# SyncE gathers seven tiles of each edge stage row by row

## The reference, cut to what matters

```python
k = typed_linear(x, ntype, Wk).reshape(n, H, HS)      # q and v alike
k_j, q_i, v_j = (k[src], q[dst], v[src])
kw = rel_apply(k_j, etype, Watt)                      # per head and relation, 16x16
a = (kw * q_i).sum(-1) * pri[:, etype].T / SQRT_D
amax = jax.ops.segment_max(a, dst, num_segments=n)
ex = jnp.exp(a - amax[dst])
den = jax.ops.segment_sum(ex, dst, num_segments=n)
alpha = ex / (den[dst] + 1e-16)
m = rel_apply(v_j, etype, Wmsg)
agg = jax.ops.segment_sum(alpha[..., None] * m, dst, num_segments=n)
out = jax.nn.silu(typed_linear(agg.reshape(n, HID), ntype, Wa))
```

## Time and profile before

| | |
|---|---|
| median of 3 runs | 2782.73 us (2780.76 to 2786.0) |
| profiled execution | 2787.17 us, span 2785.5 us |
| GpSimd busy | 1945.5 us (70%), 2030 instructions |
| VectorE busy | 2357.5 us (85%), 5622 instructions |
| TensorE busy | 1628.5 us (58%) |
| ScalarE busy | 1296.0 us (47%) |
| first and last gather, layer 0 | 348.57 and 1328.33 us |
| first and last gather, layer 1 | 1600.28 and 2578.16 us |

### The profile page before, as it was taken

How to read it: one execution, slowest core, us unless ns; L and a number is a source line. 1 busy time by engine, 2 the same in 40 slices (tenths; PEclk the granted TensorE clock), 3 DMA queues, 4 the chain that set the end, 5 groups by cost and what they waited for, 6 DMA issues and landing times. The chain is left out here.

```text
span 2785.5 us, 49119 instructions
## 1 busy us (share of the span) xinstructions
PE 1628.5 (58%) x11035; PEld 1427.7 (51%) x11035; DVE 2357.5 (85%) x5622; ACT 1296.0 (47%) x4592; POOL 1945.5 (70%) x2030
## 2 busy tenths in 40 slices
PE   1967645555555555555577645555555555556466
PEld 1855535555555555454455545555554555555344
DVE  7977679888898888888578689888898888988588
ACT  0037614444444444444577724444444444444455
POOL 2636677777777777777377677777777777777276
PEclk6569968777778787877699967787778777777655
DMA  5539876666666666665267776666666666665311
GB/s 135 89 139 355 326 226 191 186 182 185 187 181 186 184 184 185 184 185 166 75 272 276 281 219 184 186 184 185 186 184 186 184 185 184 184 183 161 126 47 37
DMA packets 386053, 512.90 MB, mean 184 GB/s; under 512 B 74933, under 2 KB 297835, under 8 KB 373268
## 3 DMA queue, kind: packets, MB, share of 16 engines
q0 software_dynamic: 101952, 328.62, 38.0%
q1 hardware_dynamic: 274712, 179.39, 21.7%
q10 hardware_dynamic: 9104, 1.86, 0.4%
HBM read 382.63 MB, written 142.96 MB: 189 GB/s over the span
## 5 line engine op out<-in xcount | busy, mean ns | idle before, releaser
L1248 POOL DMA_INDIRECT g_rows<-node_kv,edge_key_sb x1564 | 1481.5, 947 | 483.1 <-issue 442.7
L1426 ACT ACTIVATE acc<-g_ps_sum 128x127 f32 x1564 | 414.8, 265 | 851.3 <-DVE g_gained L1360 720.0
L1430 ACT ACTIVATE acc<-acc,g_gained,g_scale x1564 | 600.0, 384 | 2.1 <-issue 1.2
L1487 PE MATMUL g_ps_q<-g_qw,g_hot_t 128*128 128x128 f32 x3128 | 544.2, 327 | 83.3 <-DMA g_qw<-node_q 48.2
L1476 PE MATMUL g_ps_sum<-g_hot,g_rows 128*128 128x128 f32 x3128 | 565.6, 338 | 1.4 <-ACT acc L1430 1.4
L1487 PEld LDWEIGHTS g_ps_q<-g_qw,g_hot_t 128*128 128x128 f32 x3128 | 496.5, 239 | 96.3 <-DMA g_qw<-node_q 49.4
L1476 PEld LDWEIGHTS g_ps_sum<-g_hot,g_rows 128*128 128x128 f32 x3128 | 535.6, 256 | 2.0 <-ACT acc L1430 1.9
L1282 DVE TENSOR_TENSOR g_rows<-g_rows,g_ps_q 128x512 f32<-128x512 f32 (+1 forms) x446 | 256.9, 618 | 96.2 <-DMA g_rows<-node_kv,edge_key_sb 95.0
L1496 PE MATMUL g_ps_a<-ident,g_score 128*112 128x128 f32 x112 | 51.4, 459 | 418.4 <-DVE g_score L1287 418.4
L1496 PEld LDWEIGHTS g_ps_a<-ident,g_score 128*112 128x112 f32 x112 | 18.8, 168 | 443.6 <-DVE g_score L1287 443.6
L1262 DVE TENSOR_TENSOR g_hot_t<-g_rank_row,g_ps_a 128x1792 f32<-128x1792 bf16 x112 | 224.7, 2006 | 23.8 <-DMA g_rank_row<-edge_rank 23.5
(11 more groups left out here) (249 smaller groups left out, 2872.4 us busy)
## 6 DMA issues: line engine op xcount, KB each, us to landing
g_qw<-node_q SPq DMA_DIRECT2D x1564, 64.0 KB
g_rank_row<-edge_rank SPq DMA_DIRECT2D x110, 448.0 KB
g_rows<-node_kv,edge_key_sb POOLq DMA_INDIRECT x1564, 3.2
node_agg<-n_agg SPq DMA_DIRECT2D x24, 256.0 KB, 2.3
node_rows<-node_x SPq DMA_DIRECT2D x2, 1792.0 KB
node_q<-l_blank_q SPq DMA_DIRECT2D x1, 3200.0 KB
node_q<-n_q_sb,node_slot POOLq DMA_INDIRECT x112
node_kv<-n_kv,node_id POOLq DMA_INDIRECT x112
```

What stands on the lines that cost most here:

```text
L1248: g_.indirect_dma_start(out=rows[b % U][:, g, :], out_offset=None, in_=scratch["kv"][:, :], in_offset=bass.IndirectOffsetOnAxis(ap=tab["ke ...
L1426: a.activation(acc[:, bass.ds(w + 1, P - 1)], ps_sum[q % BANKS][:, n, 1:P], ACT.Copy).then_inc(s["copied"], 1)
L1430: a.activation(at, at, ACT.Identity, scale=scale[b % 2][:, 0, g:g + 1], bias=gained[q % BANKS][:, n:n + 1]).then_inc(s["joined"], 1)
L1487: ins = t.matmul(ps_q[q % BANKS][:, n, :], hot_t[b % 2][:, g, :], qw[b % 2][:, g, :], start=True, stop=True)
```

## The change

In each edge stage seven tiles, the last (tile 13) of batches 6, 14, 22, 30, 38, 46 and 54, are no longer gathered by GpSimd. SyncE fetches their rows one DMA per row, 128 x 7 = 896 DMAs of 1 KB for a layer, with addresses from registers: 40 rows in batch 0, 16 in each batch after it, and 8 in batch 54. The rows go to two tiles of their own (`far0`, `far1`); when a tile is complete, SyncE copies it into its place in `rows` with one more DMA, at the start of the following call of `batch`. VectorE's product of tiles 12 and 13 waits for that copy in those batches.

The keys of the seven tiles and a second copy of the window starts are put in partitions 64 and 32 of `window_starts_sb` in the tables stage, and GpSimd scales them there to offsets in bytes. SyncE's query DMAs now use the byte offsets and a view of `node_q` as bytes.

```diff
@@ tables stage, SyncE @@
-                sp.dma_start(tab["w0"][:, :], scratch["w0"].rearrange("(p w) -> p w", p=1)).then_inc(s["rows_in"], 16)
+                sp.dma_start(tab["w0"][0:1, :], scratch["w0"].rearrange("(p w) -> p w", p=1)).then_inc(s["rows_in"], 16)
+                sp.dma_start(tab["w0"][Q_AT:Q_AT + 1, :], scratch["w0"].rearrange("(p w) -> p w", p=1)).then_inc(s["bytes_in"], 16)
+                far_keys = edge_key[0:FAR * FAR_STEP * G * P].rearrange("(j t e) -> j t e", j=FAR, e=P)[:, FAR_FIRST * G + FAR_TILE, :]
+                sp.dma_start(tab["w0"][KEY_AT:KEY_AT + 1, :].rearrange("o (j e) -> o j e", e=P), far_keys.rearrange("(o j) e -> o j e", o=1)).then_inc(s["bytes_in"], 16)
@@ tables stage, GpSimd, at its end @@
+                pool.wait_ge(s["bytes_in"], 32)
+                g.tensor_scalar(tab["w0"][Q_AT:Q_AT + 1, :], tab["w0"][Q_AT:Q_AT + 1, :], float(4 * D), None, ALU.mult)
+                g.tensor_scalar(tab["w0"][KEY_AT:KEY_AT + 1, :], tab["w0"][KEY_AT:KEY_AT + 1, :], float(8 * D), None, ALU.mult)
@@ constants @@
+Q_AT, KEY_AT = 32, 64
+FAR = 7
+FAR_TILE = G - 1
+FAR_HEAD, FAR_ROWS = 24, 16
+FAR_DONE = tuple(min(FAR * P, FAR_HEAD + FAR_ROWS * (b + 1)) for b in range(BATCHES))
+FAR_OF = tuple(min(b for b in range(BATCHES) if FAR_DONE[b] >= (j + 1) * P) for j in range(FAR))
@@ edge stage, SyncE @@
+                def far_rows(at, n):
+                    sp.reg_load(key_regs[0:n], tab["w0"][KEY_AT:KEY_AT + 1, at:at + n])
+                    for k in range(n):
+                        j, p = (at + k) // P, (at + k) % P
+                        if p == 0 and j >= 2:
+                            sp.wait_ge(s["far_put"], 16 * (j - 1))
+                        key = sp.snap(key_regs[k], min_val=0, max_val=8 * D * (N * R - 1))
+                        sp.dma_start(far[j % 2][p:p + 1, :].bitcast(U8), kv_bytes[bass.ds(key, 8 * D)].rearrange("(o w) -> o w", o=1)).then_inc(far_in[j % 2], 16)
+
+                def far_tile(b):
+                    if b in FAR_OF:
+                        j = FAR_OF.index(b)
+                        sp.wait_ge(far_in[j % 2], 16 * P * (j // 2 + 1))
+                        sp.wait_ge(s["sums"], GROUP[b - U] + FAR_TILE // FOUR + 1)
+                        sp.dma_start(rows[b % U][:, FAR_TILE, :], far[j % 2][:, :]).then_inc(s["far_put"], 16)
@@ its batch(b) @@
                     if b >= 2:
                         sp.wait_ge(s["spread"], GROUP[b - 1])
-                    for g in range(SIZES[b]):
-                        w = windows(sp, regs, b, g)
-                        sp.dma_start(qw[b % 2][:, g, :], scratch["q"][bass.ds(w, P), :]).then_inc(q_in[b % 2], 16)
+                    if b >= 1:
+                        far_tile(b - 1)
+                    at, n = FIRST[b] // G * NB, SIZES[b]
+                    sp.reg_load(regs[0:n], tab["w0"][Q_AT:Q_AT + 1, at:at + n])
+                    for g in range(n):
+                        w = sp.snap(regs[g], min_val=0, max_val=4 * D * N)
+                        sp.dma_start(qw[b % 2][:, g, :].bitcast(U8), q_bytes[bass.ds(w, 4 * D * P)].rearrange("(p w) -> p w", p=P)).then_inc(q_in[b % 2], 16)
                     if b + 1 < BATCHES:
                         sp.wait_ge(s["hot_t"], b + 1)
                         ranks(b + 1)
+                    done = FAR_DONE[b - 1] if b > 0 else 0
+                    for at in range(done, FAR_DONE[b], FAR_ROWS):
+                        far_rows(at, min(FAR_ROWS, FAR_DONE[b] - at))
@@ edge stage, GpSimd @@
+                        if b in FAR_OF and g == FAR_TILE:
+                            continue
@@ edge stage, VectorE, products(b, k) @@
+                    if k == FAR_TILE // FOUR and b in FAR_OF:
+                        dve.wait_ge(s["far_put"], 16 * (FAR_OF.index(b) + 1))
```

More of the change, by code:

```diff
@@ L21 @@
 I32 = mybir.dt.int32
+U8 = mybir.dt.uint8
 ALU = mybir.AluOpType
@@ L1153 @@
 GROUP = tuple(sum(len(fours) for fours in FOURS[:b]) for b in range(BATCHES + 1))
+Q_AT, KEY_AT = 32, 64
[4 more added lines that the diff above has]
+FAR_OF = tuple(min(b for b in range(BATCHES) if FAR_DONE[b] >= (j + 1) * P) for j in range(FAR))
+FAR_FIRST, FAR_STEP = FAR_OF[0], 8
+assert FAR_OF == tuple(FAR_FIRST + FAR_STEP * j for j in range(FAR)) and FAR_OF[-1] < BATCHES - 1 and FAR * P == B * NB
 UNTIL = tuple(FIRST[b] + four[-1] + 1 for b in range(BATCHES) for four in FOURS[b])
@@ L1171, in edge_stage @@
         rows = [sb(f"rows{j}", [P, G, 2 * D]) for j in range(U)]
+        far = [sb(f"far{u}", [P, 2 * D]) for u in range(2)]
         qw = [sb(f"qw{u}", [P, G, D]) for u in range(2)]
@@ L1204, in loaded @@
         def loaded(b, late):
-            return 16 * sum(max(n - EARLY, 0) if late else min(n, EARLY) for n in SIZES[b % U:b + 1:U])
+            return 16 * sum(max(SIZES[n] - (n in FAR_OF) - EARLY, 0) if late else min(SIZES[n], EARLY) for n in range(b % U, b + 1, U))
         def windows(engine, regs, b, g):
@@ L1218, in _ @@
                 regs = [sp.alloc_register(f"sp_window{l}_{k}") for k in range(G)]
+                key_regs = [sp.alloc_register(f"sp_key{l}_{k}") for k in range(FAR_ROWS)]
+                far_in = [s[f"far_in{u}"] for u in range(2)]
+                q_bytes = scratch["q"].rearrange("n d -> (n d)").bitcast(U8)
+                kv_bytes = scratch["kv"].rearrange("n d -> (n d)").bitcast(U8)
+                def far_rows(at, n):
[12 more added lines that the diff above has]
+                        sp.dma_start(rows[b % U][:, FAR_TILE, :], far[j % 2][:, :]).then_inc(s["far_put"], 16)
                 def ranks(b):
@@ L1542, in gnn @@
                    seam=sb("seam_flags", [GH, B, P + 1], BF16),
-                   w0=sb("window_starts_sb", [1, B * NB], I32), new=sb("tile_new_sb", [H, T], BF16),
+                   w0=sb("window_starts_sb", [KEY_AT + 1, B * NB], I32), new=sb("tile_new_sb", [H, T], BF16),
                    id=sb("node_id", [P, TT], I32), slot=sb("node_slot", [P, TT], I32), sum_row=sb("node_sum_row", [P, TT], I32), type=sb("node_type", [P, TT, TN], BF16))
```

## The result

| | before | after |
|---|---|---|
| median of 4 runs | 2783.45 us (2780.76 to 2786.0) | 2803.05 us (2800.15 to 2805.28) |
| ratio after / before | | 1.0064, interval 1.0051 to 1.0077 |
| profiled execution | 2787.17 us, span 2785.5 us | 2800.15 us, span 2798.4 us |
| first and last gather, layer 0 | 348.57, 1328.33 us | 349.80, 1336.84 us |
| first and last gather, layer 1 | 1600.28, 2578.16 us | 1607.84, 2590.26 us |

The change makes the kernel slower by 17.8 us by the ratio (14 to 21); the two medians lie 19.6 us apart, inside that interval. The forecast was +4.7 us inside a range of -6 to +43: the sign is right, the size is not. By the two profiled executions the difference is 12.9 us; that of after was the fastest of its four runs and that of before was slower than all four of its, so the spans show where the time goes and understate how much it is.

What follows compares the result with a forecast made beforehand. GpSimd was taken to bound both edge stages: -17.5 us for 14 gathers and +22.2 us for layer-start stalls gave +4.7 us, 2787.4 us on a median of 2782.7, range 2777 to 2826.

Steps and rivals of the forecast that it cites:

- The bound and the gain: Edge stages: GpSimd is the bound; leaving out 14 gathers of 1.253 us brings -17.5 us.
- The start of a layer: Batch 0's 40 rows delay the first sums; GpSimd stalls at batch 3, 13.6 and 8.6 us, together +22.2 us.
- the delay: Start of a layer: 40 rows and three loads make the rank row of batch 2 19.5 us later (12.9 to 22.9).
- GpSimd's time to spare: First gather of batch 3: GpSimd asks for the sums 5.9 us (layer 0) and 10.6 us (layer 1) after they ended.
- SyncE's pace: Steady state of the edge stages: SyncE's period 16.96 us per batch (14.3 to 18.3), fitting within GpSimd's 17.38.
- threshold: Edge stages: SyncE, starting 19.5 us late, sets the pace only if its period is above 17.14 us per batch.
- rival A: Edge stages: SyncE becomes the pacer, VectorE waiting for rank rows; +43 us at a 17.5 us period; chance 0.31.
- Parts that cost nothing: Tables stage's extra DMAs and two GpSimd operations, hidden under 29 us of cover; also tile copies, semaphores and DMA-engine load.
- The other signs: Expected profile: 775 gathers a layer 1.25 us apart; batch 2's rank row issued near 395.5, used near 401.
- rival C: VectorE's product of a copied tile: the far tile is late, its wait replacing the gather's; 0.02 with anything else.

Runs made afterwards that it cites:

- skip_only: Kernel before with byte tables and byte queries; GpSimd leaves out the fourteen tiles and nobody fetches them (output differs): ratio 0.9987.
- late_dve: Changed kernel with six far tiles a layer, rows only from batch 3 on, and the two multiplications on VectorE instead of GpSimd: 0.9947 of before, -14.8 us.
- bytes_only: Kernel before plus only the byte tables and byte queries, GpSimd multiplying; no far rows, GpSimd gathers every tile: ratio 1.0045, +12.5 us.
- fill_only: Kernel before plus a fill of a spare tile and added waits on GpSimd, without a multiplication: ratio 0.9992.
- bytes_dve: bytes_only with its two multiplications on VectorE instead of GpSimd: ratio 1.0000 to the kernel before.
- after_dve: The whole changed kernel with the two multiplications on VectorE instead of GpSimd: ratio 1.0022 to the kernel before, +6.1 us.
- burst_only: bytes_only plus the 40 row DMAs of batch 0 in each layer and none later; GpSimd gathers every tile: ratio 1.011, 18 us more than bytes_only.
- early_op: fill_only plus a one-word GpSimd multiplication at the start of the tables stage, ahead of its indirect DMAs: ratio 0.9995 to the kernel before.

## Why the prediction was right and wrong

**The bound and the gain: right.** GpSimd bounds the edge stages, and a tile that it leaves out is worth a gather: 16 us for 14 (skip_only), 14.8 for 12 (late_dve).

**The start of a layer: right in its chain, a sixth too large.** Forecast 13.6 + 8.6 = 22.2 us, measured 11.2 + 7.8 = 19.0, ended by the sums as the text said and only at the first gather of batch 3. The rank rows of batches 1 and 2, layer 0 of before first, then layer 1 of before and of after (those of batch 2 in before are in the earlier trace rows):

```profile
366.11 0.42 SPq L1222 DMA_DIRECT2D g_rank_row<-edge_rank  x1
...
1611.99 0.42 SPq L1222 DMA_DIRECT2D g_rank_row<-edge_rank  x1
```

```profile
1618.18 0.42 SPq L1259 DMA_DIRECT2D g_rank_row<-edge_rank  x1
...
1646.88 0.43 SPq L1259 DMA_DIRECT2D g_rank_row<-edge_rank  x1
```

From one to the other it took 394.80 - 366.49 = 28.31 us in layer 0 against 9.91 before, 18.4 more, and 28.70 in layer 1 against 9.00, 19.7 more. The forecast had 19.5, so the delay was sized well, if with cheaper rows and dearer loads than assumed. The mis-sized term is GpSimd's time to spare, 5.9 and 10.6 us, read from the trace of before as if GpSimd kept its place beside SyncE. In layer 0 it is ready for batch 3 at 403.30 + 0.95 + 0.30 = 404.55, 1.5 us later than the 403.02 of before; in layer 1 it is 7.8 us later than before while the rank row of batch 1 is only 6.2 later. That is 1.5 us a layer; the rest is the delay of layer 0, 1.1 us too large.

**SyncE's pace: its work as forecast by luck, the margin gone.** The forecast had a period of 16.96 us and a threshold of 17.14. The rows were cheaper: a group of 16 takes 6.13 us in most batches, (6.13 - 0.23) / 15 = 0.393 a row, not 0.42. The loads were dearer: 1.164 for 16 words where 0.90 was taken, and the load of the query offsets, which now stands behind the rows, went up to a median of 1.425 from 1.167. SyncE's groups in the middle of layer 0:

```profile
807.12 0.43 SPq L1259 DMA_DIRECT2D g_rank_row<-edge_rank  x1
808.93 6.13 SPq L1248 DMA_DIRECT2D g_far<-node_kv  x16
816.70 7.15 SPq L1270 DMA_DIRECT2D g_qw<-node_q  x14
823.91 0.42 SPq L1259 DMA_DIRECT2D g_rank_row<-edge_rank  x1
```

16.8 us in this batch. The mean is longer, because some query DMAs stall (up to 1.845 us each). From the rank row of batch 2 at 394.80 to that of the last batch,

```profile
1309.71 0.42 SPq L1259 DMA_DIRECT2D g_rank_row<-edge_rank  x1
```

are 914.91 us for 53 batches, 17.26 each. Take off the 0.30 of waiting and 16.96 is left, the forecast's value, reached by errors that cancel. The signs that the text gave for rival A are there: the rank row is what VectorE waits for (27.6 us in 30 of the batches between 403 and 1314 us), and the wait for gathered rows is nearly gone. The last rank row is issued 27.1 us ahead of the layer's last gather, where it was 38.9 in the kernel before (1328.33 - 1289.47).

Yet A costs little. The threshold follows from how late SyncE starts and how late the layer ends. With the measured values, the rank row of batch 2 18.8 us later (394.80 - 376.02) and the last gather 8.5 us later (1336.84 - 1328.33), the forecast's own formula gives 17.42 - (18.8 - 8.5) / 53 = 17.23, an estimate; 17.26 is 0.03 above it, 1 to 2 us in 53 batches. The ends of the layers agree. In the four kernels without rows that were read (before, bytes_only, fill_only, bytes_dve) the last group of products starts 5.4 to 6.3 us after the last gather of its layer. In after it is 5.9 and 6.7, in after_dve 6.7 and 8.4. In the timelines of VectorE, layer 1 of after and of after_dve:

```profile
2596.93 1.88 DVE L1330 TENSOR_TENSOR g_rows<-g_rows,g_ps_q 128x512 f32<-128x512 f32 x3
```

```profile
2587.26 1.88 DVE L1330 TENSOR_TENSOR g_rows<-g_rows,g_ps_q 128x512 f32<-128x512 f32 x3
```

So SyncE's pace is worth 0 to 2 us at the end of a layer, not the 19 of rival A at 17.5 us. The slow gathers even helped here: they gave SyncE 0.1 us more per batch (14 x 7.4 ns).

**"Parts that cost nothing": the step that failed.** The two GpSimd operations of the tables stage were costed by their cover: "29 us of cover; without it they would cost a few us once". The cover is there and the operations fit into it. What was wrong is the question. The row of the gather was carried over as "unchanged at 1.25 us apart", as if its duration were a constant of the instruction; it went to 1.258, and 7 ns times 1564 is 11 us, on the very engine that bounds the kernel. The added operations were the only change to what GpSimd does outside the gathers, and nothing in the trace of before showed an arithmetic operation of it between indirect DMAs, so its cost could not be read off that trace and should have had a bound above nothing. Why such an operation lengthens later gathers stays open.

**How the terms add up.** From the profiles and runs: -17.5 for the gathers, +19.0 for the stalls, +12.2 for GpSimd's late operations (the mean of 12.5, 12.3 and 11.7), +1 to +3 for SyncE's pace, in all +15 to +17; measured 17.8 (14 to 21). Without the third term it is +2.5 to +4.5, and after_dve measured +6.1 (0.3 to 12). The forecast's +4.7 was therefore about the right sum of an incomplete list, and in part by luck: 3.2 us too much for the stalls stand against 1 to 3 left out for SyncE's pace. That the range held the result is luck, too: its upper part was there for rival A, and what filled it was the slow gathers.

**The other signs.** There are 775 gathers in a layer, 1.258 us apart and not 1.252. The rank row of batch 2 and VectorE's use of it came at 394.80 and 399.87, near the 395.5 and 401 of the forecast. VectorE's waits ahead of its products are for gathered rows (5.9 us) and for the spread queries (2.4 us), none for the copied tile, and SyncE waits for far rows twice in the kernel, 3.6 us in all (rival C did not come). The Trainium skill, page "DMA: Bandwidth & Descriptors", section "Rules for kernel authors", would merge such small transfers; here 16 of them in a batch were issued 0.39 us apart and landed in time for every tile but those two waits, so their fixed costs overlapped, and what they cost was SyncE's time to issue them.

The prediction took a row to run on a single DMA engine, which no run had shown by then. The page's line for queue q1, in which SyncE's DMAs are counted, of bytes_only and then burst_only with its 80 rows (packets, MB, share):

```profile
q1 hardware_dynamic: 274728, 179.40, 21.5%
q1 hardware_dynamic: 274888, 179.48, 21.3%
```

160 packets and 0.08 MB more for 80 rows of 1 KB: two packets a row, one of which carries the whole row (the other has 4 B in the trace). So the row isn't split over engines; whether all rows share one engine the traces don't say.

## What to carry over

Cost an added instruction by what it does to the instructions after it on the engine that bounds, not only by its own duration and cover; where a duration is multiplied by 1564, give it a bound of a per cent. Here the remedy was to give GpSimd's multiplications to VectorE (bytes_dve) or to run them ahead of its first indirect DMA (early_op); other kinds of operation were not tried. Work that is spread evenly over a pipeline must not begin with a lump in the first batch: 40 small DMAs ahead of the rank row of batch 2 cost 19 us, and in late_dve the rows that begin in batch 3 cost nothing that can be measured (-14.8 us for 15.0 of gathers).

## What the runs showed of the hardware

One GpSimd multiplication of a single word (0.37 us) after GpSimd's first indirect DMAs lengthens the later edge gathers from 942 to 949 ns at the least and from 946 to 953 at the median, and this lasts to the last gather, 2.4 ms later. The gathers of the node stages go up alike (973 to 981 ns at the median), the scatters do not (988 and 988). The same operation ahead of the first indirect DMA leaves the edge gathers at 942 and 946, and a fill ahead of it (fill_only) does, too.

A DMA of 1 KB in one run, with its address from a register, occupies SyncE for 0.228 us and comes every 0.39 us with its two moves; one of 128 rows of 512 B takes 0.333 us. A load of 16 registers takes 1.16 us, and so did the load of 14 query offsets in bytes_only, where no rows are fetched; behind a group of row DMAs the same load took 1.425. No run looked for the cause.

In bytes_only the loads read:

```profile
L1265 SPq TENSOR_LOAD <-window_starts_sb x112: 754/1168/1414, 359.8 to 2557.5; - x112
```
